# Third attention of a four-layer gated cross-attention kernel: P V issued in three groups of heads, with V's two projections between them

## The reference, cut to what matters

```python
x = x + jnp.tanh(g_xattn[2]) * _L2_xattn_ref(_layernorm(x, axis=-1), ctx_1024, ctx_1024, mask_BxSxS2_bf1, ...)

def _L2_xattn_ref(queries, keys, values, masks, Wq, bq, Wk, bk, Wv, bv, Wo, bo):
    q = (queries @ Wq + bq).reshape(B, S, H, dk).transpose(0, 2, 1, 3)
    k = (keys @ Wk + bk).reshape(B, S, H, dk).transpose(0, 2, 1, 3)
    v = (values @ Wv + bv).reshape(B, S, H, dv).transpose(0, 2, 1, 3)
    scores = jnp.einsum('bhqd,bhkd->bhqk', q, k) / jnp.sqrt(jnp.float32(dk))
    scores = jnp.where(masks[:, None, :, :], scores, jnp.float32(-1000000000.0))
    attn = jax.nn.softmax(scores, axis=-1)
    out = jnp.einsum('bhqk,bhkd->bhqd', attn, v)
    cat = out.transpose(0, 2, 1, 3).reshape(B, S, VALUE_DIM)
    cat = cat.transpose(0, 2, 1).reshape(B, S, VALUE_DIM)
    return cat @ Wo + bo
```

## Time and profile before

| | us |
|---|---|
| median of 3 runs (lowest, highest) | 2752.37 (2749.81, 2772.16) |
| the profiled execution's own time | 2753.38 |
| its span, first to last instruction | 2751.6 |
| third attention, steps with P V and no L446 (steps 8 to 16, starts of P V) | 1484.4 to 1566.8 |
| third attention, steps with P V and L446 (steps 17 to 37, starts of P V) | 1576.9 to 1841.6 |

### The profile page before, as it was taken

One profiled execution on the slowest core, in us unless ns is written; L12 is line 12 of the kernel. 1 busy time (PEld: TensorE's weight loads), 2 busy tenths in 40 slices (PEclk: granted clock), 3 DMA queues, 4 the chain that ended last, 5 costly groups with the idle time before them and its releaser, 6 DMA issues. The chain is left out here.

```text
span 2751.6 us, 77920 instructions
## 1 busy us (share of the span) xinstructions
PE 2249.3 (82%) x32227; PEld 1705.9 (62%) x32227; DVE 1791.9 (65%) x4725; ACT 1351.5 (49%) x2507; POOL 1217.9 (44%) x1731
## 2 busy tenths in 40 slices
PE   4999999999959599945648999983888848888597
PEld 3888888887747377734435766662555526666465
DVE  3777777777733488858866766644444458888544
ACT  2555555555513288829964544430111148777332
POOL 1333333434435411127751244445455566777535
PEclk9999999999979799976668988875899967677699
DMA  6112100000035211100000111111444322222263
GB/s 172 58 62 81 66 26 26 25 22 21 18 116 169 65 59 55 48 17 1 1 26 29 33 41 42 41 33 68 135 133 135 108 68 69 81 85 74 82 181 112
DMA packets 212353, 184.49 MB, mean 67 GB/s; under 512 B 33356, under 2 KB 187542, under 8 KB 212000
## 3 DMA queue, kind: packets, MB, share of 16 engines
q1 hardware_dynamic: 192544, 142.51, 17.6%
q0 software_dynamic: 19456, 36.99, 3.8%
HBM read 102.01 MB, written 72.68 MB: 63 GB/s over the span
## 5 line engine op out<-in xcount | busy, mean ns | idle before, releaser
L446 POOL DMA_INDIRECT slots<-row,put x256 | 264.4, 1033 | 251.0 <-issue 100.7
L1777 PE MATMUL experts_H<-experts_xs_t,experts_w 128*128 128x512 f32 x576 | 274.6, 622 | 26.5 <-DVE experts_xs_t L1702 22.3
L1649 POOL DMA_INDIRECT rows<-experts_y,experts_idx x160 | 155.4, 971 | 133.4 <-DVE experts_y L1726 88.1
L964 ACT ACTIVATE l_prob_t<-l_Z 128x512 f32<-128x512 f32 x256 | 132.2, 603 | 156.4 <-PE l_Z L1087 125.7
L1795 PE MATMUL experts_Y<-experts_w,experts_hid 128*128 128x128 f32 x1664 | 198.9, 276 | 10.3 <-DVE experts_y L1726 7.0
L1321 POOL TENSOR_TENSOR l_var_eps<-l_mv,eps 128x1 f32<-128x1 f32 x64 | 12.1, 189 | 430.9 <-DVE l_mv L1403 430.9
L1795 PEld LDWEIGHTS experts_Y<-experts_w,experts_hid 128*128 128x128 f32 x1664 | 192.4, 192 | 13.1 <-issue 13.1
L1777 PEld LDWEIGHTS experts_H<-experts_xs_t,experts_w 128*128 128x128 f32 x576 | 109.0, 200 | 142.1 <-issue 112.1
L878 DVE TENSOR_REDUCE l_top<-l_X 128x32 f32<-128x2048 f32 x64 | 146.6, 2290 | 72.8 <-PE l_X L1096 51.2
L1360 DVE TENSOR_REDUCE l_top<-l_S 128x16 f32<-128x1024 f32 x64 | 78.3, 1223 | 165.9 <-PE l_S L1499 165.9
L762 POOL TENSOR_TENSOR l_var_eps<-l_mv,eps 128x2 f32<-128x2 f32 x96 | 25.2, 262 | 333.1 <-DVE l_mv L860 228.2
(11 more groups left out here) (327 smaller groups left out, 5987.0 us busy)
## 6 DMA issues: line engine op xcount, KB each, us to landing
experts_w<-in_F_w SPq DMA_DIRECT2D x104, 256.0 KB
l_ctx_t<-in_ctx_t SPq DMA_DIRECT2D x96, 128.0 KB, 2.3
l_q_m<-l_q_t SPq DMA_DIRECT2D x384, 32.0 KB, 1.8
experts_xs<-slots SPq DMA_DIRECT2D x40, 264.0 KB
slots<-l_empty SPq DMA_DIRECT2D x16, 536.0 KB
experts_xs<-slots SPq DMA_DIRECT2D x16, 536.0 KB
slots<-l_empty SPq DMA_DIRECT2D x16, 520.0 KB, 5.1
experts_xs<-slots SPq DMA_DIRECT2D x16, 520.0 KB
```

The costliest lines, as they stand in the source:

```text
L446: pool.indirect_dma_start(self.slots, bass.IndirectOffsetOnAxis(ap=g.put[c][:, tile:tile + 1], axis=0), g.row[:, tile, self.sent_cols], No ...
L964: nc.scalar.activation(prob_t[:, t.par(PROB), r, :], Z[:, r, :], ACT.Exp).then_inc(prob_done, 1)
L1649: pool.indirect_dma_start(rows, bass.IndirectOffsetOnAxis(ap=idx[:, t.par(4, XS), k:k + 1], axis=0), y[:, t.par(4), k, :], None, bounds_ch ...
L1777: nc.tensor.matmul(H[:, c, :], w1_s[:, t.par(2), c, :], xs_t[:, t.par(2), :], start=True, stop=True).then_inc(h_filled[c], 1)
```

## The change

P V's loop becomes a function over a range of heads, `o_of_heads`. In steps where PROB and OUT are both live, and in the third attention alone, PE waits for ACT's read of bank 2 ahead of V's first projection, issues heads 0 to 5 (24 records), V's first projection, heads 6 to 11 (24 records), V's second projection with `xv_filled`, and then heads 12 to 15 (16 records) with `o_filled`. Before, V's bias and both projections with `xv_filled` came first, and then all 64 records. V's bias stays ahead of everything. The wait for bank 2 stands ahead of both of the first two groups (at the second it is passed already). Step 39 and the other attentions keep the old order.

```diff
+            def o_of_heads(t, first, end):
+
+                term = soft if stable else prob_t
+                for h in range(first, end):
+                    for tile in range(2):
+                        col = 256 * tile + 64 * (h % 4)
+                        last = nc.tensor.matmul(O[64 * tile:64 * tile + 64, 18 * h:18 * h + 18], term[:, t.par(OUT), h // 4, col:col + 64],
+                                                val[:, t.par(OUT), tile, h, :, :].rearrange("p b c -> p (b c)"), start=True, stop=True)
+                return last
...
                         for tile in range(2):
+                            if folded and t.live(OUT):
+                                bank_read(t, 2)
+                                o_of_heads(t, 6 * tile, 6 * tile + 6)
                             last = nc.tensor.matmul(XV[:, 256 + P * tile:256 + P * tile + P], ctx_t[:, t.par(PROB, SLOTS_CTX), P * tile:P * tile + P],
                                                     wv_s[:, :], start=not folded, stop=not folded or tile == 1)
                     last.then_inc(xv_filled, 1)
...
-                    else:
+                    elif not folded or not t.live(PROB):
                         bank_read(t, 2)
-                    term = soft if stable else prob_t
-                    for h in range(16):
-                        for tile in range(2):
-                            col = 256 * tile + 64 * (h % 4)
-                            last = nc.tensor.matmul(O[64 * tile:64 * tile + 64, 18 * h:18 * h + 18], term[:, t.par(OUT), h // 4, col:col + 64],
-                                                    val[:, t.par(OUT), tile, h, :, :].rearrange("p b c -> p (b c)"), start=True, stop=True)
-                    last.then_inc(o_filled, 1)
+                    o_of_heads(t, 12 if folded and t.live(PROB) else 0, 16).then_inc(o_filled, 1)
```

## The result

The changed kernel takes 2781.78 us (median of 10 runs, 2768.86 to 2799.61), the kernel before 2754.03 (10 runs, 2737.29 to 2772.16). The ratio is 1.0107, interval 1.0081 to 1.0133: slower, by 22 to 37 us. The profiled execution of the changed kernel is the fastest of its runs, 2768.86 us, so the two traces differ by 15.5 us only, and the medians by 27.8. The granted clock of each execution was taken as well: 0.868 in the profiled one, as in the kernel before's, and 0.855 to 0.865 in the other nine. Over the whole program a typical execution of the changed kernel so spends some 45 us more at 1.2 GHz than its trace shows.

The account below looks back on a forecast made before the run. PE was taken to bound the kernel, with breaks in its instruction supply and a lowered clock beside L446. Crossings 3 us plus break 4 us gave +7, 2760.6 for the profiled execution, about 2760 as median; range 2708 to 2785.

Parts of the forecast that it names:

- rival B: Third attention: bubbles pull PE's clock down in steps 8 to 16 that keep it now; +50 us, 2802; chance 0.22.
- Three crossings, 0.3 us a step: Three more switches between 128x64 and 128x128 work on PE, counted in the ten steps without a break: 3 us.
- The break goes by the count: P V beside L446: break stays after the same record count, +0.6 us a step; +0.2 taken, 4 us over 21 steps.
- the rule that spoke against the change: Tiling-mode changes drain TensorE; by that alone the change could only lose, 31 x 0.3 = 9 us, 2762.
- the refill: V's pairs between P V groups let PE's instruction supply catch up, leaving fewer records behind the break: -0.6 us a step.
- I leave it where it is, and the clock with it.: Steps with L446: the break's end hangs on POOL, not PE's order, so its end and the clock stay unchanged.
- Rival A: P V beside L446: the break goes, wholly or mostly, and the clock stays up; 2692 or 2715; chance 0.28.
- The covers: Bank 2 wait has 0.6 us cover, costs nothing; V's copies on ACT come 0.2 to 0.3 us later, still hidden.

Follow-up runs that it names:

- e3: Changed kernel with two groups instead of three: heads 0 to 5, both of V's projections, heads 6 to 15; 2657.39 us, 1.0024 of the kernel before.
- f3: Changed kernel with four groups instead of three, V's bias also put between groups of P V; 2804.78 us, 1.0105 of the kernel before.
- f1: The kernel before, unchanged, run again in the second set for its trace; 2788.93 us in its one run.
- f2: The changed kernel, unchanged, run again in the second set; 2805.27 us, 1.0081 of the kernel before.
- e2: Changed kernel with POOL's scatter L446 moved one step later, behind o_filled; 2688.87 us, 1.0145 of the kernel before.
- e1: Kernel before, old order of P V, with POOL's scatter L446 moved one step later, behind o_filled; 2662.58 us, 1.0046 of the kernel before.
- g2: Changed kernel with POOL's last-step L446 put between its normalisation work and the router's variance and root; 2694.27 us, 1.0140 of the kernel before.
- g1: Kernel before with POOL's last-step L446 put between its normalisation work and the router's variance and root; 2654.89 us, 1.0013 of the kernel before.
- g3: The kernel of e1 run again, in the third set; 2661.75 us, 1.0025 of the kernel before.
- e4: Changed kernel with all 64 P V records in one run and both of V's projections behind them; 2654.90 us, 1.0007 of the kernel before.
- g4: The kernel of e3 run again, in the third set; 2658.74 us, 1.0023 of the kernel before.
- f4: Changed kernel with one 128x128 by 128x256 matmul more ahead of V's bias, which overwrites it; 2804.72 us, 1.0081 of the kernel before.

## Why the prediction was right in its direction and short in its size

I had forecast 2760, +7 us on a median of 2752.4, with a range of 2708 to 2785. Measured 2781.78 against 2754.03, so +28. That is inside the stated range, and in part by luck: it lies outside the forecast's own 2745 to 2775, just past the 1% (27 us) that I had called no change, and beyond the 2780 from which rival B was to decide. The range held it because half of B was in it.

- *Three crossings, 0.3 us a step.* Right in kind, small in size: 0.42 us for the three, with e3 showing 0.11 for one. By 31 steps 13 us instead of 9. The drain that the Trainium skill's "TensorEngine Tiling (Array Packing)", Key Properties, names for a change of tiling mode agrees with this, at 0.11 to 0.14 us a crossing (0.06 for f3's further two); it was the rule that spoke against the change.
- *The break goes by the count.* Right in that it stays, and only roughly as a count. V's records taken in, 36 to 55 records pass before it in the changed kernel and 37 to 58 in the kernel before, and the number goes with L446's place (f1). The idle time under "issue" is still there, 13.4 us against 20.2 in the first pair of traces and 14.3 against 17.8 in the second. I take that fall for the refill; no run isolates it. Set against the crossings (8.8) it leaves a loss of 2 and 5 us in the 21 steps, where I had 4, so the term's size came out although its two parts were guessed. The Trainium skill's "TensorE: Matmul & The Clock Gate", in the table at its head, gives TensorE a queue 64 instructions deep. An estimate from that figure is 32 records with their loads. The fewest of P V's records that pass in f1, 31, are near that, but the most are 52, and a group of 24, which would fit, wasn't safe. No trace shows what stands in the queue. A few steps do go without a break (two of 21 in the changed kernel's first trace, five in f2, two in f1).
- *"I leave it where it is, and the clock with it."* This is the step that failed. The window from step 17, forecast at 281 to 286 us and 0.8, took 293.3 at 0.77. In the 21 steps the changed kernel spends 28 us more at 1.2 GHz (135 against 107) and f2 19 more than f1; at 0.36 us each that is 10 and 7 us. Over whole executions the clocks show 44 us more in f2 than in the kernel before. Without breaks it is worse: 49 us more in the 21 steps of e2 than in e1's, 39 more in g2's than in g1's, 18 and 14 us at that rate.
- *Rival B's place.* B had the clock falling in steps 8 to 16. In the condition of the first measurement it doesn't: both kernels have 0.96 there. It falls in the 21 steps. Without breaks it does fall there too, to 0.93 in e2 and g2 from 0.96 and 0.98, some 2 to 4 us. So B's mechanism is the one that was missing from the forecast's sum, in another place and at a third of its price.
- *Rival A.* Nothing of it came that lasts: the steps that lose their break are too few, and the 21 steps as a whole lose clock, 0.77 against 0.81 and 0.76 against 0.78.
- *The covers.* Both held. ACT's L988 ends 1 us ahead of PE's next step, and the wait for bank 2 costs nothing that shows in P V's start.

The sum with measured terms, for the first pair of traces: 3.3 in the nine steps; in the 21, 8.8 for crossings, 10 for the clock and -6.8 for idle time, 12.0 against 12.8 measured. With the nine steps that is 16.1 us in the third attention, where the spans differ by 15.5. Of the 27.8 us between the medians the other 12 have no place in a trace, since the only trace of the changed kernel from that measurement is of its fastest run. The clocks say what they may be: the 45 us more at 1.2 GHz of a typical execution are worth 11 to 17 us at 0.25 to 0.38. That they fall in the third attention isn't shown. The other stages differ by several us in either direction from run to run.

What stays open: what the condition with breaks is, whether L446 is needed for a break there (g1 was made to test it and met the other condition; for it speaks that none of the nine steps without L446 breaks in any trace, and that the break moves with L446), what the changed kernel loses without breaks where L446 stays in its place, and what decides when the clock falls.

## What to carry to other kernels

Put between groups of narrow matmuls, wide ones cost a crossing each way, 0.11 to 0.14 us here, and on an engine without slack that is paid in full in each step. Price a change in PE's order by its clock as well: multiply the time at 1.2 GHz, read from the granted clock of the stretch, by what such a microsecond costs (0.29 and 0.36 us in the two pairs here), since that term was as large as the work added, or twice it. And run the kernel before beside each change: its own time moved by 5% with the condition that it met, five times the effect in question.

## What the runs showed of the hardware that I had not expected

The same program took 2648, 2652, 2754 and 2780 us in four measurements. Of the 100 to 130 us between them, 50 to 70 lie in the 21 steps with L446: 281 and 286 us with breaks, 215 to 230 in the kernels e1, g1, g3 and e4, which have the 64 records in one piece, without. L446 beside P V isn't enough for a break: e3, e4, e1 and g4 have it beside P V in most steps and none breaks in the way of the first trace. The feed-forward block behind the third attention is slower in the condition with breaks too: from its first to its last L1777 record 262 and 274 us (the first trace, f1) against 225 (g3, e4). From 1890 us on PE waits 52.8 us in f1 for the loads of the experts' rows (experts_xs from slots), and 19.6 in g3. So P V is only one place where it shows. Why is not known.

Dense work added where PE was thought thin (f4) did not keep the level at 2.4 GHz in the one trace of it: in the nine steps it is 0.89 against 0.96. Over all executions the two kernels' clocks, 0.861 and 0.857, are too near each other to tell.
